# Mixing of three batches in split f32r products, with spilled residual rows

## The reference, cut to what matters

```
x = L0_attn_x                                        # (4, 2048, 256)
x = layernorm(x + attention(x))                      # x1, masked scores without a softmax
# soft mixture of experts, E = 16 experts of S = 16 slots, H = 64
xn      = layernorm(x1, gamma, beta)
logits  = einsum('bnd,des->bnes', l2norm(xn) * scale, l2norm(mu))
dispatch = softmax(logits, over tokens n)            # routing
combine  = softmax(logits, over all 256 slots)
slot_in  = einsum('bnd,bnes->besd', xn, dispatch)
h        = gelu(einsum('besd,edh->besh', slot_in, w1) + b1)
slot_out = einsum('besh,ehd->besd', h, w2) + b2
out      = einsum('besd,bnes->bnd', slot_out, combine)   # mixing
return layernorm(x1 + out)
```

## Time and profile before

| what | us |
|---|---|
| median of 3 runs | 590.18 (590.04 to 590.53) |
| the profiled execution, its own time | 590.34 |
| its span | 588.6 |
| PE busy / DVE / ACT / POOL | 572.5 / 485.6 / 393.4 / 393.9 |
| routing, from the first exponentials to the last fold | about 399 to 514 |
| experts' stage | about 514 to 525.5 |
| mixing on PE | 525.5 to 581 |
| PE's busy share of the span | 97% |
| TensorE's granted clock, mean | 0.996 of full speed |

### The profile page before, as it was taken

The page is one execution under the profiler, slowest core; times in us unless marked ns, Lnnn a source line. Parts: engine busy times, 40 slices in busy tenths (PEclk is TensorE's granted clock), DMA queues, the critical chain, the costliest instruction groups (busy, mean ns, idle before and its releaser), DMA issues. The chain is left out here.

```text
span 588.6 us, 11698 instructions
## 1 busy us (share of the span) xinstructions
PE 572.5 (97%) x3796; PEld 528.0 (90%) x3796; DVE 485.6 (83%) x1048; ACT 393.4 (67%) x855; POOL 393.9 (67%) x395
## 2 busy tenths in 40 slices
PE   9999999999999999999999999979999999999994
PEld 7889989999999999999998999968999999888883
DVE  6579889899898898888989989979988777557885
ACT  4765666676766667667677666567688777435765
POOL 0869779789797797787977978785646443104453
PEclk9999999999999999999999999999999999999998
DMA  8324134043141331422403403105555555923445
GB/s 234 81 73 108 22 87 99 12 107 43 65 107 18 89 71 41 102 33 74 107 13 94 86 23 74 26 11 98 84 72 72 73 73 73 147 33 108 143 144 179
DMA packets 163473, 47.04 MB, mean 80 GB/s; under 512 B 139470, under 2 KB 159340, under 8 KB 163436
## 3 DMA queue, kind: packets, MB, share of 16 engines
q1 hardware_dynamic: 163424, 46.57, 36.9%
q10 hardware_dynamic: 12, 0.00, 0.0%
HBM read 21.39 MB, written 8.39 MB: 51 GB/s over the span
## 5 line engine op out<-in xcount | busy, mean ns | idle before, releaser
L523 POOL TENSOR_TENSOR h_lo<-xn_all,h_hi 128x512 fp32r<-128x512 f32 x32 | 41.4, 1295 | 68.2 <-ACT xn_all L649 67.1
L647 ACT ACTIVATE h_hi<-bank,bias_col 128x512 fp32r<-128x512 f32 x96 | 66.4, 692 | 18.8 <-PE bank L793 17.1
L791 PE MATMUL bank<-xnT_hi,w_hi 128*128 128x512 f32 x188 | 76.2, 405 | 0.0
L792 PE MATMUL bank<-xnT_lo,w_hi 128*128 128x512 f32 x188 | 74.4, 396 | 0.0
L793 PE MATMUL bank<-xnT_hi,w_lo 128*128 128x512 f32 x188 | 74.2, 395 | 0.0
L682 ACT CAST state_hi<-bank 128x512 fp32r<-128x512 f32 x57 | 33.5, 588 | 50.1 <-PE bank L926 50.1
L1608 PE MATMUL bank<-xn_all,e_tok 128*128 128x257 f32 x256 | 65.1, 379 | 0.0
L1190 DVE TENSOR_TENSOR state_lo<-bank,state_hi 128x512 fp32r<-128x512 f32 x57 | 39.4, 691 | 29.0 <-ACT state_hi L682 29.0
L1686 PE MATMUL bank<-w_sb,ET_all 128*128 128x256 f32 x256 | 55.4, 379 | 0.0
L1686 PEld LDWEIGHTS bank<-w_sb,ET_all 128*128 128x128 f32 x256 | 48.6, 190 | 6.6
L1507 ACT ACTIVATE e_tok<-bank,shift,xinv 128x256 f32<-128x256 f32 x64 | 36.1, 565 | 27.3 <-PE bank L1598 20.5
(11 more groups left out here) (202 smaller groups left out, 2081.6 us busy)
## 6 DMA issues: line engine op xcount, KB each, us to landing
x_all<-in_L_attn_x SPq DMA_DIRECT2D x16, 512.0 KB, 3.9
kT<-k_turn SPq DMA_DIRECT2D x128, 64.0 KB, 2.5
ET_all<-e_turn SPq DMA_DIRECT2D x64, 128.0 KB, 3.8
xn_all<-in_xT SPq DMA_DIRECT2D x15, 512.0 KB, 4.7
out<-xn_all SPq DMA_DIRECT2D x15, 512.0 KB, 3.0
w_sb<-in_L_ffn_w SPq DMA_DIRECT2D x2, 512.0 KB, 5.3
xn_all<-in_L_ffn_w SPq DMA_DIRECT2D x2, 512.0 KB, 6.6
xn_all<-in_xT SPq DMA_DIRECT2D x2, 256.0 KB, 3.5
```

The lines of the kernel that those rows point to most:

```text
L523: pool.tensor_tensor(h_lo[:, V_SLOT, m, :], hv[:, m, :], h_hi[:, V_SLOT, m, :].bitcast(F32), ALU.subtract).then_inc(hv_split, 1)
L647: nc.scalar.activation(h_hi[:, h_slot(j, n), m, :], ps, ACT.Gelu, bias=bias(n, m))
L791: nc.tensor.matmul(ps, w[0], xs[0], start=start, stop=False, skip_group_check=shared)
L792: nc.tensor.matmul(ps, w[0], xs[1], start=False, stop=False, skip_group_check=shared)
```

## The change

The mixing of batches 1, 2 and 3 (groups 4 to 15) goes in split f32r products: six products a tile where there were two float32 ones. Batch 0 (groups 0 to 3) stays as it was. For that, the exponentials and the experts' output are needed as `hi` and `lo`:

- `ET_hi` lies over `x1_all` (the same addresses), `ET_lo` over `ET_all`. ACT rounds a group of 128 x 1024 (`round_e`), POOL subtracts (`split_e`). Groups 4 to 12 are split in routing, on ACT behind the exponentials of a group's last tile, on POOL behind `add_beta`; groups 13, 14 and 15 in the experts' stage.
- Since `ET_hi` overwrites x1, the x1 of groups 4 to 15 is written to DRAM in routing (`spill_x1`, 512 KB a group, ahead of an exchange on SP) and read again (`reload_x1`): groups 4 to 7 behind the last exchange, into `e_turn` and `xnT_hi1`'s place, groups 8 to 15 during the mixing of groups 0 to 7, into the places of `ET_all` that have been used.
- ACT writes `so_hi` for batches 1 to 3; DVE subtracts `so_lo` (three of 128 x 512) ahead of the first sums.

```diff
+                def spill_x1(g):
+                    sp.wait_ge(tok_scaled, GT * g)
+                    n = g - FIRST
+                    if n > 1:
+                        sp.wait_ge(x1_spilled[n % 2], 16 * (n // 2))
+                    sp.dma_start(x1_spill[n], x1_all[:, GT * g:GT * g + GT, :]).then_inc(x1_spilled[n % 2], 16)
+                def reload_x1(g):
...
+                    sp.dma_start(x1_again[g], x1_spill[n]).then_inc(x1_reloaded[n % 2], 16)
                 for g in range(GROUPS):
+                    if g + GB - 1 in SPLIT_GROUPS:
+                        spill_x1(g + GB - 1)
                     exchange_e(g)
...
+                for g in range(FIRST, AGAIN):
+                    reload_x1(g)
                 for k in range(LAST):
+                    if k + AGAIN in SPLIT_GROUPS:
+                        reload_x1(k + AGAIN)
                     sp.wait_ge(y_normed, GT * k + GT)
...
+                def split_e(g):
+                    pool.wait_ge(e_rounded, g - FIRST + 1)
+                    exact = ET_all[:, g, :, :]
+                    pool.tensor_tensor(ET_lo[:, g, :, :], exact, ET_hi[:, g, :, :].bitcast(F32), ALU.subtract
+                                       ).then_inc(e_split, 1)
...
+                    if t % GT == GT - 1 and k - 3 in SPLIT_GROUPS and not (last and q == 0):
+                        round_e(k - 3)
+                def round_e(g):
+                    n = g - FIRST
+                    act.wait_ge(e_moved[g % 2], 16 * FOUR * (g // 2 + 1))
+                    act.wait_ge(x1_spilled[n % 2], 16 * (n // 2 + 1))
+                    nc.scalar.copy(ET_hi[:, g, :, :], ET_all[:, g, :, :]).then_inc(e_rounded, 1)
...
+                for n in SO_ORDER:
+                    dve.wait_ge(so_ready, n + 1)
+                    nc.vector.tensor_tensor(so_lo[n - SPLIT[0]],
+                                            so_ps[n][:, :].rearrange("p (s d) -> p s d", s=SB),
+                                            so_hi[:, n, :, :].bitcast(F32), ALU.subtract).then_inc(so_split, 1)
```

More of the change, by code:

```diff
@@ L1341, in build @@
             slot_inT = msb("slot_inT", [P, KB, B, ES])
+            so_lo = [place[:, :, :].rearrange("p k (h d) -> p (k h) d", d=D)[:, SB * i:SB * i + SB, :]
+                     for place in (xnT_hi[0], xnT_lo[0]) for i in range(2)]
+            with nc.sbuf_tensor("so_hi", [P, B, SB, D], F32R) as place:
+                so_hi = place
             w1_sb = msb("w1_sb", [P, KB, E, H])
@@ L1457, in route @@
                             add_beta(pool, GB * b + q + 3, (q + 3) % GB)
+                        if GB * b + q - 2 in SPLIT_GROUPS and not (last and q == GB - 1):
+                            split_e(GB * b + q - 2)
                         if b == 0 and q == 2:
@@ L1547, in _ @@
                 route(B - 1, last=True)
+                round_e(GROUPS - GB + 1)
+                round_e(GROUPS - GB + 2)
                 for half in range(2):
```

69 lines of the change are left out of this document (64 added, 5 removed).

## The result

The changed kernel takes 585.82 us in the median of 6 executions (585.07 to 586.92), the kernel before on the same chip 590.32 (589.94 to 591.02, 6 executions). The ratio is 0.9924, with a 95% interval of 0.9914 to 0.9935: faster by 4.5 us where the forecast was 6.5 (583.7), and inside the range. The profiled execution of the changed kernel takes 585.22, its span is 583.7.

A forecast was written before the change was run, and what follows sets the result against it. PE, busy 97% of the span, was taken as the bound. From the profiled 590.34 us, -7.2 for mixing, +0.5 for experts and +0.2 for routing and transfers gave 583.8, median 583.7; range 582.7 to 587.0, chance 0.85.

The forecast's parts named there:

- Step 1: Mixing, groups 4 to 15: products at 0.1167 us each, so a group takes 2.80 us in place of 3.455.
- Step 2: Mixing: DVE's own work, the ACT-POOL-DVE loop and POOL's own loop each need 2.75 us a group, under PE's 2.80.
- Step 3: Mixing: group 15 gains nothing, so eleven groups gain 0.655 us each, -7.2 us (-6.5 at 2.86 a group).
- Step 4: Experts' stage: two ACT roundings of 1.0 us ahead of the table load make gelu late, +0.5 us.
- Steps 5 and 6: Routing: ACT's nine roundings cost 0 to +0.2 us in all; POOL's subtractions of 2.19 to 2.71 us fit idle time.
- Step 7: Routing and mixing: spills, reloads and stores cost nothing, +2 at the other end; +0.2 us added for routing and transfers.
- Rival E: Mixing: weight loads do not hide in a long run, 4.56 us a group, 603 us; chance 0.02.
- A: Mixing: the forecast itself, PE at 2.80 to 2.86 us a group, 582.9 to 584.6 us; chance 0.53.
- B: Mixing: DVE's loop of dependent steps becomes the bound at 2.85 to 3.0 us a group, 585.0 us; chance 0.20.
- C: Mixing: stores behind reloads are late, sums of groups 8 to 11 wait, +1 to +2.5, 585.5 us; chance 0.09.
- D: Routing: ACT or POOL is late by 0.2 to 0.4 us in nine groups, 586.5 us; chance 0.07.
- F: Routing: the spill holds up the exchange and DVE waits; 593 us at 4.2 us a spill; chance 0.04.

## Why the prediction was right, and where it was off

- **What bounds the kernel.** Right, and still so: PE is full in mixing before and after.
- **Step 1, the products.** The kind of the gain was right, its size was the step that was off: a product takes 0.1185, not 0.1167. A group is 2.844 in place of 2.80, and the gain 11 x 0.611 = 6.7, as measured, in place of 7.2. The length of the run, which the prediction named as the risk, is not the reason. Inside the logits' short runs the products came at the same distance before the change, five steps in 508.04 - 507.45 = 0.59:

```profile
507.45 0.28 PE L1597 MATMUL bank<-mu_lo,xnT_hi 128*128 128x256 f32 x1
...
507.92 0.28 PE L1598 MATMUL bank<-mu_hi,xnT_lo 128*128 128x256 f32 x1
508.04 1.03 PE L1608 MATMUL bank<-xn_all,e_tok 128*128 128x257 f32 x4
```

  Over 63 such runs of the kernel before a step is 0.1188 in the mean. The 0.1167 is a difference of two rounded rows, 1.57 - 0.87, for a tile that was one of the shortest (the median is 1.574, and four records of the fold are 0.866: 0.118 a product). Nor does w1's row show the pace: 3.81 / 32 = 0.119 has the whole last record in it, and its starts, 515.72 to 519.25, lie 0.114 apart. That the bound of 0.119 came so near was luck.
- **Step 2, whether others keep up.** DVE's own 2.75 was right (2.73 measured). That the rings also need only 2.75 was wrong, for a reason that no row of before could show. They hold only as long as DVE's shift is issued ahead of POOL's addition. With PE at 2.84, ACT's scaling ends at 558.27 and the addition starts at 558.35, 0.04 behind the shift. With PE faster, or once PE is ahead, the addition can start first, and a group is 3.20 where it does. Whether a group of 2.80 would have kept the order was not measured; the shortest group in which the shift went through right beside the addition took 2.82, once, in the run with four products.
- **Step 3.** Right: eleven groups gained, and the last store's issue follows the sums of group 15 by 4.99 in both.
- **Step 4, the experts' stage.** Right to 0.01: +0.49, a rounding of 1.0, gelu behind the load. The undoing of it gave the 0.49 back. (The prediction's rows make gelu 519.27 - 518.69 = 0.58 late, not 0.55; nothing hangs on it.) POOL's three subtractions took 2.35 to 2.36 each, the last until 525.2, and DVE's sums of the first group started at 528.96, with nobody waiting for them later.
- **Steps 5 and 6, ACT and POOL in routing.** Right: with all of this work and no transfers routing takes 119.24 against 119.25. The subtraction took 2.38 in the mean, between the bounds of 2.19 and 2.71.
- **Step 7, transfers.** Mis-sized. Nine profiles with the spills in their place have routings of 119.43 to 120.24, 119.74 in the mean: +0.5 and not +0.2, for the turns' waits. The failed piece is "its buffer is wanted 8.8 us after that": the turn that waited until 450.90 had been ready at 450.14, 6.8 us behind the exchange's first issue (443.31), of which SP took 3.8 to issue the four quarters. And a spill behind an exchange makes it land at 7.0 to 7.8 in place of 6.3 to 6.6, so that it crosses those 6.8. And the sum had no term for the end of the kernel, where the reloads cost 0.55.
- **The rule on weight loads** of the Trainium skill, "TensorE: Matmul & The Clock Gate", "The mechanism": the trace doesn't agree here. Each of the 24 products of a group has a load of the whole array, 0.19 us long, and the products still start every 0.1185. Rival E falls.
- **The rule on the table** of the Trainium skill, "ScalarE: Activation LUTs", "What ACT_TABLE_LOAD costs": its 1283 ns agree (1.28), its drain of 1380 ns does not show. Gelu starts at 519.89, the load began at 518.60.
- **Rivals.** A has the mechanism (a group of 2.84, within its 2.80 to 2.86), but its times, 582.9 to 584.6, miss the median of 585.82: the range held by the room left for B, C and D, none of which shows in the profile. B (DVE's ring at 2.85 to 3.0) gives nearly the measured time, and is not what happened; the runs with less work on POOL, ACT and DVE rule it out. C (sums waiting for a store) is absent in the profile of the changed kernel and present in three others (waits of 0.7 to 1.2 us, once a kernel). F is present in small, and in full where a wait in SP's queue made it so.

**The sum with measured terms:** -6.7 for mixing, +0.5 for the experts' stage, +0.5 for routing in the mean, +0.55 at the end: -5.15. The profiled execution became 5.12 shorter, but that agreement is chance: in it routing gave only +0.18, so that its stretches without attention add up to -5.44, and attention's +0.54 and 0.2 us outside the span make up the rest. The medians say -4.5 and -4.8 in two comparisons of the same kernel. The 0.3 to 0.6 between them and the sum is not explained. Attention, whose thirteen profiles have a mean 0.24 above the one of before, may be a part of it; so may a store's wait in some executions and the 3.20 that follows it, which the executions without a profile don't show.

**The best version** of the kernels that leave nothing out is the one with the moved roundings: 584.72 against 590.29 before. Its lead over the changed kernel, 0.49 in the trace, is smaller than the medians' scatter. A further gain in mixing would need the shift out of the addition's way first; the one place tried for it costs more than it saves (3.05 a group, with four products a tile).

## What to carry to other kernels

When an engine becomes faster until the others have no idle time, "never idle" says no longer who sets the pace, nor does the chain that ended last, which named DVE here. Count the steps of the engine that you made faster, and see whether its instructions stand without a pause. Take work away from each suspect, one at a time, before believing in a ring; three such runs changed the answer here. And size a repeated instruction by the distance of neighbouring starts inside a run, over many runs. A difference of two rounded rows, and a row's length divided by its count, were off by 0.04 and 0.12 us a group, and the forecast rested on a margin of 0.05.

## What the runs showed of the hardware

**A small DVE instruction can be held up by POOL for the whole of POOL's instruction.** The shift (two SBUF operands, 128 x 4) takes 0.16 when it starts 0.04 ahead of POOL's addition (128 x 256, two SBUF operands), and 0.60 to 0.65 when it starts 0.01 to 0.06 behind it; it then ends with the addition. In all profiles together it got through in 0.15 to 0.17 each time that it started 0.04 to 0.11 ahead; of 26 starts up to 0.06 behind, 23 were held up, and in the other three, all in the run with four products, the addition took 0.67 to 0.69 in place of 0.64. The statistics, with one SBUF operand, run beside the same addition at 0.70. The Trainium skill, "SBUF — State Buffer", section "Who interferes with whom", says that a DVE instruction with two SBUF inputs and a GpSimd one that reads SBUF exclude each other, whichever starts first. The trace agrees, and shows what it does to a pipeline: the shift loses 0.44 to 0.49 us and the group goes from 2.84 to 3.20, decided by hundredths of a microsecond.

**A faster engine made the kernel slower.** With PE at 1.90 us of work a group the groups took 3.20, with PE at 2.84 they took 2.84, since at PE's pace ACT's scaling ends late enough to keep the addition behind the shift.

**A transfer is late for its neighbours on the queue by its issue as well as by its bytes.** A spill issued behind an exchange makes that exchange land about 1 us later (7.0 to 7.8 us in place of 6.3 to 6.6). SP needs 3.77 us to issue one exchange of 512 KB in four parts, and 0.8 for a spill directly behind it (0.35 when the exchange has landed). Where the next exchange is due, all that stands ahead of it on the queue delays it: 9.64 us of spills made the first exchange start at 410.17 in place of 407.8 to 408.0, and DVE wait 2.67 us.
